# ScalarE instead of VectorE blanks the sums of two graph attentions, and the count stores are issued one group sooner

## The chip, the cores and the metric

The kernel runs on one core of one Trainium2 chip. The metric is the device time of one execution in microseconds (us). A core has TensorE (PE in the rows), VectorE (DVE), ScalarE (ACT), GpSimd (POOL) and SyncE (SP), each with its own instruction stream; they wait for each other on semaphores. Transfers run on 16 DMA engines, and here they are issued by SP (dense copies) and by POOL (gathers of single rows by an index).

## The reference, cut to what matters

Four graph networks run one after the other on the same 3125 nodes of 256 numbers, each followed by a residual sum and a layer norm. The first two are attentions over 53125 edges, sorted by their target node. For the first one, with `row` the source and `col` the target of an edge:

```python
scores = jnp.sum(Q[col] * (K[row] + rel), axis=-1) / np.sqrt(DK)
m = jax.ops.segment_max(scores, col, num_segments=N)
e = jnp.exp(scores - m[col])
denom = jax.ops.segment_sum(e, col, num_segments=N)
out = jax.ops.segment_sum((e / denom[col])[:, :, None] * V[row], col, num_segments=N)
x = _layernorm(x + out.reshape(N, 256) @ Wo.T + bo)
```

The second attention takes its scores from one number per node, head and side (`alpha_src[src] + alpha_dst[dst]`, then a leaky ReLU) instead of a product of rows, and has the same softmax and sums. The third and fourth network (five and three layers) sum over the same edges; this kernel does that as a product with a dense 3125 x 3125 matrix that counts the edges between each pair of nodes.

## The kernel before, in words

Both attentions are one function, `attend_edges`, called with `layer` 0 and 1. The edges stand in 416 chunks of 128, and eight chunks are a group, so there are `NG` = 52 groups. One turn of the loop over groups is called a tick here. For a group:

- POOL gathers the source rows of its 1024 edges, one indirect transfer per chunk, into one of four buffers (`from_src`, line 827). It may run ahead until all four buffers are in use.
- SP loads eight windows of target rows (`window`, line 807), two buffers. Ahead of each eight it reads eight start offsets into registers (line 800). From the third group on it also waits until PE has used the buffer.
- PE spreads the windows over the edges by a product with a one-hot matrix (`spread_windows`, line 987). VectorE turns the result into scores: in attention 0 it multiplies (`match`, line 850) and reduces (line 858), in attention 1 it reduces and adds the gathered part (`take_scores`, from line 864). Then it scans for the peaks (876, 879), builds the one-hot matrix of two groups later (840, 841), and subtracts (`shift_scores`, 889, 892).
- ScalarE takes the exponential (`weigh`, 1101, 1102). VectorE weights the rows by it (`weigh_rows`, 897, one tick later), and PE sums the 128 rows of each chunk (`sum_parts`, 1017, 1019) into one of three PSUM banks. ScalarE copies each bank into `sums` at the chunk's offset (`copy_sums`, line 1120) and the last two columns into `ends` (1122).

`sums` is 3 planes of 3712 columns, on 128 partitions. Chunks write 128 columns each at run-time offsets and may leave columns out, so `sums` has to be blank before the first copy. In attention 1 it lies in a part of `room`, and the rows show it by that name. Line 940 blanks it as one instruction on VectorE, after the first two one-hot matrices and some smaller memsets and ahead of the first scores.

Attention 1 also makes the count matrix (`adj`), in ticks 0 to 49. VectorE makes one-hot matrices of windows (`spot_windows`, 929, 931), PE multiplies them one tick later (1032), and ScalarE copies 160 results into `counts`, a buffer of two halves (1135). Sixteen halves are written in all. SP stores each to `adj` (line 795), and ScalarE waits before the first copy of a half until the store of the half two before it has landed. SP stands in the order of its loop: the windows of group g, then `store_halves(g)`, which issues the store of each half that falls to g:

```python
done = next(t for t in range(NG) if HG * (half + 1) <= NWG * (t + 1) // TICKS)
if g == min(NG - 1, done + 5):
```

`done` is the tick in whose turn VectorE makes the last one-hot matrices of the half. The halves come every three ticks, now and then four, and the last two are both issued at g = 51. An attention ends when every engine has passed a barrier; SP passes it when all stores have landed.

Of the kernel before, what the change touches and what calls it, by code (L numbers as in the profile page):

```python
# [11 lines left out]
ACT = mybir.ActivationFunctionType  # L12
AX_X = mybir.AxisListType.X

P = 128
# [3 lines left out]
KH = D // P  # L19
# [5 lines left out]
C = 416  # L25
G = 8
NG = C // G
# [3 lines left out]
PBUF = PARTS + P  # L31
# [50 lines left out]
def sems(nc, ctx, *names):  # L82

    made = [nc.alloc_semaphore(name=n) for n in names]
    ctx.used += made
    return made
# [619 lines left out]
def attend_edges(nc, keep, layer, by_src, by_part, ws, wd, scale, adj=None):  # L706
# [7 lines left out]
    with Phase(nc) as ctx:  # L714
# [57 lines left out]
        win_in = sems(nc, ctx, *(f"e{layer}_win_in{b}" for b in range(2)))  # L772
        spread = sems(nc, ctx, *(f"e{layer}_spread{s}" for s in range(2)))
        used = sems(nc, ctx, *(f"e{layer}_used{s}" for s in range(2)))
        whole_copied, blank = sems(nc, ctx, f"e{layer}_whole_copied", f"e{layer}_blank")
        spotted, counted, copied = sems(nc, ctx, *(f"e{layer}_{n}" for n in ("spotted", "counted", "copied")))
        half_out = sems(nc, ctx, *(f"e{layer}_half_out{i}" for i in range(2)))
        block = ctx.enter_context(nc.Block(f"edges{layer}"))
# [4 lines left out]
        def width_of(half):  # L783
            return AN - HALF if half % 2 else HALF

        @block.sync
        def _(sp):
            def store_halves(g):

                for half in range(NHALF):  # L790
                    done = next(t for t in range(NG) if HG * (half + 1) <= NWG * (t + 1) // TICKS)
                    if g == min(NG - 1, done + 5):
                        sp.wait_ge(copied, HG * (half + 1))
                        at = half % 2 * HALF
                        sp.dma_start(adj[half // 2][:, :, at:at + width_of(half)],
                                     counts[:, half % 2, :, 0:width_of(half)]).then_inc(half_out[half % 2], 16)

            def load_windows(it, b, again):
                g = RING * it + b
                starts = [sp.value_load(keep["offset"][0:1, bass.ds(g * G + j, 1)], min_val=0, max_val=PARTS) for j in range(G)]  # L800
                if again and layer == 0:

                    sp.wait_ge(spread[1], PAIRS // 2 * (g - 1))
                elif again:
                    sp.wait_ge(spread[b % 2], RING // 2 * it + b // 2)
                for j in range(G):
                    sp.dma_start(window[:, b % 2, j, :], by_part[bass.ds(starts[j], P), :]).then_inc(win_in[b % 2], 16)

            for b in range(RING):
                load_windows(0, b, b >= 2)  # L810
            for g in range(RING, NG):
                load_windows(g // RING, g % RING, True)
                if counting:
                    store_halves(g)
            if counting:
                for i in range(2):
                    sp.wait_ge(half_out[i], 16 * (NHALF // 2))
# [14 lines left out]
        def _(v):  # L832
# [104 lines left out]
            nc.vector.memset(small[:, :, :, COL_SIZE:SMALL], 1.0).then_inc(zeroed, 1)  # L937
            for s in range(BANKS):
                nc.vector.memset(part_ps[s][COL_SIZE:P, KH * ENDS:(KH + 1) * ENDS], 0.0).then_inc(blank, 1)
            nc.vector.memset(keep["sums"][:, :, :], 0.0).then_inc(zeroed, 1)  # L940
            v.wait_ge(zeroed, 3)
            if layer == 0:
                for pair in range(PAIRS):
                    match(0, pair)
# [143 lines left out]
        def _(act):  # L1088
            act.sem_inc(hot_copied, 1)

            def copy_turned(g):
                r = g % 2
                act.wait_ge(hot_turned, g + 1)
                nc.scalar.activation(onehot_t[:, r, :, :], hot_ps[:, :].rearrange("p (j e) -> p j e", j=G),
                                     ACT.Copy).then_inc(hot_copied, 1)

            def weigh(g):
                r = g % 2
                act.wait_ge(shift_done, g + 1)
                by_head = shifted[:, r, :].rearrange("p (j h) -> p j h", h=H)  # L1100
                nc.scalar.activation(share(r), by_head, ACT.Exp, scale=scale).then_inc(prob, 1)  # L1101
                nc.scalar.activation(small[:, r, :, 0:H], by_head, ACT.Exp, scale=scale).then_inc(prob_kept, 1)
# [42 lines left out]
            def tick_alpha(g):  # L1145
                copy_sums(g - 2, range(4, G))
                copy_counts(g - 1, 0, 1)
                copy_sums(g - 1, (0, 1))
                copy_counts(g - 1, 1, 2)
                if g + 2 < NG:  # L1150
                    copy_turned(g + 2)
                copy_sums(g - 1, (2,))
                copy_counts(g - 1, 2, 3)
                weigh(g)
                copy_sums(g - 1, (3,))
                copy_counts(g - 1, 3, 4)

            copy_turned(0)
            copy_turned(1)
            act.wait_ge(zeroed, 3)  # L1160
            for g in range(NG):
                if layer == 0:
                    tick_rows(g)
                else:
                    tick_alpha(g)
            copy_sums(NG - 2, range(4, G))
            copy_sums(NG - 1, range(G))

# [1957 lines left out]
```

## Time and profile before

| | |
|---|---|
| time, median of 3 runs | 2911.0 us (2905.76 to 2912.67) |
| profiled execution | 2911.57 us, span 2909.8 us |
| busy: PE, VectorE, ScalarE, POOL | 2641.3, 1567.8, 1086.8, 970.0 us |
| granted clock of TensorE, mean share | 0.956 |
| moved by DMA | 470.22 MB, 162 GB/s on the mean |

The profile is one execution; its span is what the trace covers, and 1.8 us of the time lie around it. Times in rows are us from the start of the span. A row of the timeline reads: start, duration, engine, line, operation, output<-inputs, shape, count, and in brackets how long the engine had been idle and what ended that. A duration can overlap the next instruction by some tens of ns.

### The profile page before, as it was taken

What the parts mean: (1) busy time and instruction counts of PE and PEld (TensorE: products, weight loads), DVE (VectorE), ACT (ScalarE), POOL (GpSimd) and SP (SyncE); (2) the same over time, 40 slices, a digit from 0 to 9 for tenths busy, and PEclk for the clock granted to TensorE, in tenths of its full rate; (3) what the DMA queues carried; (4) which work ended last, traced back from release to release, by engine and by line L of the source; (5) the groups of instructions that cost most, each with busy time, mean ns of one, the idle gap of its engine ahead of it and who ended that gap; (6) DMA issues with size and microseconds to landing.
All of it is one profiled execution on the core that took longest, in us unless ns stands there. A gap on an engine that the chain in (4) does not pass through costs nothing. (4 is left out here: it accounts for less than half of the span.)

```text
span 2909.8 us, 53292 instructions
## 1 busy us (share of the span) xinstructions
PE 2641.3 (91%) x17214; PEld 1918.8 (66%) x17214; DVE 1567.8 (54%) x2779; ACT 1086.8 (37%) x3021; POOL 970.0 (33%) x1020
## 2 busy tenths in 40 slices
PE   6789999998747888888799999999999989999998
PEld 4679999997636777777455555655556556565654
DVE  8689999995567888886721514215142151111123
ACT  1035555554426777776321304013040152021111
POOL 3577777772367777773400101001010000000000
PEclk8999999999769999999699999999999999999999
DMA  7799999992347988987554342543425143434342
GB/s 258 253 321 319 316 317 321 314 312 87 89 99 135 163 150 153 154 158 112 162 156 125 91 138 63 152 125 103 126 63 154 54 126 111 138 91 132 112 123 86
DMA packets 332505, 470.22 MB, mean 162 GB/s; under 512 B 155942, under 2 KB 243062, under 8 KB 331588
## 3 DMA queue, kind: packets, MB, share of 16 engines
q1 hardware_dynamic: 269364, 286.33, 38.1%
q0 software_dynamic: 59088, 176.67, 19.9%
q10 hardware_dynamic: 3776, 3.80, 0.4%
q8 instruction: 140, 2.29, 0.3%
q14 instruction: 137, 1.12, 0.1%
HBM read 412.95 MB, written 55.50 MB: 161 GB/s over the span
## 5 line engine op out<-in xcount | busy, mean ns | idle before, releaser
L2348 PE MATMUL sum_ps<-room,high 128*128 128x391 f16 x1900 | 470.3, 331 | 2.4 <-DVE z_t L2525 2.4
L2348 PE MATMUL sum_ps<-room,low 128*128 128x391 f16 x1824 | 454.1, 331 | 0.0
L827 POOL DMA_INDIRECT e_from_src<-vk,src x416 | 393.4, 946 | 141.0 <-issue 109.7
L827 POOL DMA_INDIRECT e_from_src<-val,src x416 | 393.5, 946 | 134.1 <-issue 107.3
L2746 PE MATMUL sum_ps<-room,high 128*128 128x391 f16 x1200 | 389.4, 329 | 0.5 <-DVE x L2890 0.5
L2746 PE MATMUL sum_ps<-room,low 128*128 128x391 f16 x1152 | 379.3, 329 | 0.0
L1017 PE MATMUL e_part_ps<-e_onehot,e_from_src 128*128 128x129 f32 x1664 | 288.7, 297 | 80.9 <-ACT ends L1122 71.6
L2525 DVE SCALAR_TENSOR_TENSOR z_t<-h_t,own,sum_ps 128x391 f32<-128x391 f32 x80 | 44.7, 618 | 483.9 <-PE sum_ps L2348 480.2
L1017 PEld LDWEIGHTS e_part_ps<-e_onehot,e_from_src 128*128 128x128 f32 x1664 | 225.7, 197 | 110.2 <-ACT ends L1122 97.7
L1120 ACT ACTIVATE sums<-e_part_ps 128x384 f32 x416 | 205.2, 493 | 231.1 <-PE e_part_ps L1019 203.4
L2416 POOL TENSOR_SCALAR h_t<-h_t 128x391 f32<-128x391 f32 x32 | 39.0, 1237 | 697.2 <-DVE h_t L2555 697.2
L1017 PE MATMUL e_part_ps<-x,e_from_src 128*128 128x129 f32 x1664 | 267.2, 283 | 1.7 <-DVE e_from_src L897 1.1
L2348 PEld LDWEIGHTS sum_ps<-room,high 128*128 128x128 f16 x1900 | 185.1, 98 | 126.3 <-issue 3.7
L2348 PEld LDWEIGHTS sum_ps<-room,low 128*128 128x128 f16 x1824 | 178.2, 98 | 127.7 <-issue 2.6
L2425 ACT ACTIVATE gin_y_t<-gin_proj_ps,gin_columns 128x391 f32<-128x391 f32 x80 | 47.0, 587 | 561.3 <-PE gin_proj_ps L2365 560.5
L1120 ACT ACTIVATE room<-e_part_ps 128x384 f32 x416 | 206.5, 496 | 124.4 <-PE e_part_ps L1019 59.1
L897 DVE TENSOR_TENSOR e_from_src<-e_from_src,e_fixed 128x2048 f32<-128x2048 f32 x104 | 237.3, 2282 | 15.4 <-ACT e_fixed L1101 15.4
L1017 PEld LDWEIGHTS e_part_ps<-x,e_from_src 128*128 128x128 f32 x1664 | 229.7, 191 | 20.1 <-DVE e_from_src L897 1.8
L987 PE MATMUL e_spread_ps<-e_window,x 128*128 128x256 f32 x832 | 214.4, 385 | 15.5 <-DMA e_window<-q_part 15.4
L2746 PEld LDWEIGHTS sum_ps<-room,high 128*128 128x128 f16 x1200 | 116.8, 97 | 80.3 <-issue 1.2
L987 PEld LDWEIGHTS e_spread_ps<-e_window,x 128*128 128x128 f32 x832 | 144.2, 193 | 34.2 <-DMA e_window<-q_part 12.8
L2746 PEld LDWEIGHTS sum_ps<-room,low 128*128 128x128 f16 x1152 | 112.3, 97 | 80.4 <-issue 2.1
(424 smaller groups left out, 4481.3 us busy)
## 6 DMA issues: line engine op xcount, KB each, us to landing
room<-adj SPq DMA_DIRECT2D x128, 977.5 KB, 4.8
e_window<-q_part SPq DMA_DIRECT2D x416, 128.0 KB
room<-adj SPq DMA_DIRECT2D x32, 488.8 KB
room<-adj SPq DMA_DIRECT2D x32, 391.0 KB
adj<-e_counts SPq DMA_DIRECT2D x8, 1250.0 KB
adj<-e_counts SPq DMA_DIRECT2D x8, 1193.8 KB
e_from_src<-vk,src POOLq DMA_INDIRECT x416
e_from_src<-val,src POOLq DMA_INDIRECT x416
```

What stands on the lines that cost most here:

```text
L827: nc.gpsimd.indirect_dma_start(from_src[:, b, j, :], None, by_src, bass.IndirectOffsetOnAxis(ap=keep["src"][:, g * G + j:g * G + j + 1], a ...
L897: nc.vector.tensor_tensor(from_src[:, b, :, 0:D].rearrange("p j (h d) -> p j h d", h=H), from_src[:, b, :, 0:D].rearrange("p j (h d) -> p ...
L987: mm = nc.tensor.matmul(to, onehot_t[:, r, j, :], window[:, r, j, :], start=True, stop=True)
L1017: nc.tensor.matmul(part_ps[s][:, k * ENDS:(k + 1) * ENDS], from_src[:, b, j, k * P:(k + 1) * P], onehot[:, b, j, :], start=True, stop=True)
L1120: nc.scalar.activation(keep["sums"][:, :, bass.ds(starts[j], P)], of[:, :, 0:P], ACT.Copy).then_inc(whole_copied, 1)
L2348: mm = nc.tensor.matmul(sum_ps[KH * n + m][:, 0:AN], part[:, t, m * P:(m + 1) * P], slab[s][:, n, k * AN:(k + 1) * AN], start=(t == 0 and ...
L2416: nc.gpsimd.tensor_scalar(h_t[:, 1, cols(b)], h_t[:, 1, cols(b)], 0.0, None, ALU.max).then_inc(floored, 1)
L2425: nc.scalar.activation((z_t if p else y_t)[:, m, cols(b)], proj_bank(p, v)[:, 0:AN], ACT.Identity, bias=columns[:, 3 * p, m:m + 1], scale= ...
L2525: nc.vector.scalar_tensor_tensor(out=z_t[:, m, cols(b)], in0=h_t[:, m, cols(b)], scalar=own[:, l:l + 1], in1=sum_ps[KH * n + m][:, 0:AN], ...
L2746: mm = nc.tensor.matmul(sum_ps[KH * n + m][:, 0:AN], part[:, t, m * P:(m + 1) * P], slab[s][:, n, k * AN:(k + 1) * AN], start=(t == 0 and ...
```

## The change

Blanking moves from VectorE to ScalarE, in three instructions of one plane each (`clear_sums`). They copy a zero, the last column of `once`, broadcast over 3712 columns. The first stands ahead of ScalarE's first one-hot copy, the second behind its second one, and the third at the end of tick 0, with a wait until all three are written. VectorE and ScalarE wait for two memsets instead of three. The stores of the counts are issued at `done + 4` instead of `done + 5`, so all but the last one stand one group sooner in SP's loop.

```diff
-        whole_copied, blank = sems(nc, ctx, f"e{layer}_whole_copied", f"e{layer}_blank")
+        whole_copied, blank, cleared = sems(nc, ctx, *(f"e{layer}_{n}" for n in ("whole_copied", "blank", "cleared")))
...
-                    if g == min(NG - 1, done + 5):
+                    if g == min(NG - 1, done + 4):
                         sp.wait_ge(copied, HG * (half + 1))
...
-            nc.vector.memset(keep["sums"][:, :, :], 0.0).then_inc(zeroed, 1)
-            v.wait_ge(zeroed, 3)
+            v.wait_ge(zeroed, 2)
...
+            def clear_sums(k):
+                nc.scalar.activation(keep["sums"][:, k, :], keep["once"][:, C:C + 1].to_broadcast([P, PBUF]),
+                                     ACT.Copy).then_inc(cleared, 1)
+
+            clear_sums(0)
             copy_turned(0)
             copy_turned(1)
-            act.wait_ge(zeroed, 3)
+            clear_sums(1)
+            act.wait_ge(zeroed, 2)
             for g in range(NG):
                 if layer == 0:
                     tick_rows(g)
                 else:
                     tick_alpha(g)
+                if g == 0:
+                    clear_sums(KH)
+                    act.wait_ge(cleared, KH + 1)
```

The start of attention 1 on ScalarE before the change: the one-hot copies of three groups stand together, and the first copy of counts follows the two exponentials of tick 0.

```order
L1087 UNCONDITIONAL_BRANCH
L1094 ACTIVATE e_onehot_t<-e_hot_ps 128x1024 x3
L1101 ACT_TABLE_LOAD
L1101 ACTIVATE e_fixed<-e_shifted 128x64
L1102 ACTIVATE e_small<-e_shifted 128x8x8
L1135 ACTIVATE e_counts<-e_count_ps,whole 128x25x20
```

The same place after the change (line numbers of the changed file are one less here).

```order
L1086 UNCONDITIONAL_BRANCH
L1158 ACTIVATE room<-once 128x3712
L1093 ACTIVATE e_onehot_t<-e_hot_ps 128x1024 x2
L1158 ACTIVATE room<-once 128x3712
L1093 ACTIVATE e_onehot_t<-e_hot_ps 128x1024
L1100 ACT_TABLE_LOAD
L1100 ACTIVATE e_fixed<-e_shifted 128x64
L1101 ACTIVATE e_small<-e_shifted 128x8x8
L1158 ACTIVATE room<-once 128x3712
L1134 ACTIVATE e_counts<-e_count_ps,whole 128x25x20
```

The three blanking copies now stand on ScalarE, one of them between tick 0's exponentials and its first copies out of PSUM; attention 0 has the same order without counts.

The end of attention 1 on SP before the change, behind the offsets of group 51: the last windows, then the stores of the last two halves, one behind the other.

```order
L807 ISA
L807 DMA e_window<-alpha_part 128x24
L807 ISA
L807 DMA e_window<-alpha_part 128x24
L795 DMA adj<-e_counts 3200x1x200
L795 DMA adj<-e_counts 3200x1x191
L714 UNCONDITIONAL_BRANCH
```

The place after the change to which the first of these two stores has gone: behind the windows of group 50, ahead of the offsets of group 51.

```order
L807 ISA
L807 DMA e_window<-alpha_part 128x24
L807 ISA
L807 DMA e_window<-alpha_part 128x24
L795 DMA adj<-e_counts 3200x1x200
L800 TENSOR_LOAD offset
L800 ISA x2
L800 TENSOR_LOAD offset
L800 ISA x2
```

The store of half 14 stands ahead of group 51's sixteen register reads and eight windows now; only half 15 is left at the end.

## Rows read from the trace of the kernel before

**Rows 1.** Instructions of the gathers (L827): durations ns, first and last start us.

```profile
L827 POOL DMA_INDIRECT e_from_src<-vk,src x416: 940/946/962, 133.4 to 652.3; - x139
L827 POOL DMA_INDIRECT e_from_src<-val,src x416: 941/946/992, 824.9 to 1344.1; - x139
```

**Rows 2.** Instructions of line 940, the same columns, and the idle time before them.

```profile
L940 DVE MEMSET sums<- x1: 9338/9338/9338, 139.6 to 139.6; 128x11136 f32 x1
L940 DVE MEMSET room<- x1: 9338/9338/9338, 831.1 to 831.1; 128x11136 f32 x1
...
  issue: 4.6, 2
```

**Rows 3.** Timeline of VectorE, start of attention 0 and two ticks near its end.

```profile
148.98 0.69 DVE L850 TENSOR_TENSOR e_from_src<-e_from_src,e_spread_ps 128x512 f32<-128x512 f32 x1
...
643.56 0.69 DVE L850 TENSOR_TENSOR e_from_src<-e_from_src,e_spread_ps 128x512 f32<-128x512 f32 x1 [0.65 <-PE e_spread_ps L987]
...
653.50 0.69 DVE L850 TENSOR_TENSOR e_from_src<-e_from_src,e_spread_ps 128x512 f32<-128x512 f32 x1 [0.65 <-PE e_spread_ps L987]
```

**Rows 4.** Timeline of PE, start of attention 0.

```profile
146.25 5.76 PE L987 MATMUL e_spread_ps<-e_window,x 128*128 128x256 f32 x16 [8.54 <-DMA e_window<-q_part]
...
164.18 2.07 PE L987 MATMUL e_spread_ps<-e_window,x 128*128 128x256 f32 x4 [3.85 <-DMA e_window<-q_part]
```

**Rows 5.** Timeline of SP's issues, start of attention 0: windows of group 2.

```profile
155.11 3.95 SPq L807 DMA_DIRECT2D e_window<-q_part  x8
```

**Rows 6.** Timeline of VectorE, start of attention 1.

```profile
840.51 0.36 DVE L864 TENSOR_REDUCE e_spread_score<-e_turn_ps 128x64 f32<-128x192 f32 x1
...
856.43 0.36 DVE L864 TENSOR_REDUCE e_spread_score<-e_turn_ps 128x64 f32<-128x192 f32 x1 [0.35 <-DMA e_from_src<-val,src]
```

**Rows 7.** Timeline of POOL: last gather of group 2, attention 1.

```profile
853.69 0.95 POOL L827 DMA_INDIRECT e_from_src<-val,src  x1 [0.30 <-issue]
```

**Rows 8.** Groups by line of ScalarE: count | busy us, mean ns.

```profile
L569 ACT ACTIVATE pr_part_room<-first 128x3328 bf16<-128x3328 f32 x1 | 3.0, 2977 | 2.4 <-DVE first L347 2.4
```

**Rows 9.** Timeline of ScalarE: ticks 0 and 1 of attention 0, tick 0 of attention 1.

```profile
161.50 0.25 ACT L1102 ACTIVATE e_small<-e_shifted 128x64 f32<-128x64 f32 x1
170.36 0.49 ACT L1120 ACTIVATE sums<-e_part_ps 128x384 f32 x1 [8.61 <-PE e_part_ps L1019]
...
848.12 0.24 ACT L1102 ACTIVATE e_small<-e_shifted 128x64 f32<-128x64 f32 x1
...
852.40 0.49 ACT L1120 ACTIVATE room<-e_part_ps 128x384 f32 x1 [2.36 <-PE e_part_ps L1019]
```

**Rows 10.** Timeline of SP's issues, end of attention 1.

```profile
1310.32 0.56 SPq L795 DMA_DIRECT2D adj<-e_counts  x1
...
1327.30 3.94 SPq L807 DMA_DIRECT2D e_window<-alpha_part  x8
...
1339.83 0.56 SPq L795 DMA_DIRECT2D adj<-e_counts  x1
```

**Rows 11.** Timeline of VectorE, ticks 48 to 51 of attention 1.

```profile
1325.98 0.36 DVE L864 TENSOR_REDUCE e_spread_score<-e_turn_ps 128x64 f32<-128x192 f32 x1 [0.72 <-DMA e_from_src<-val,src]
...
1344.83 0.34 DVE L864 TENSOR_REDUCE e_spread_score<-e_turn_ps 128x64 f32<-128x192 f32 x1
...
1349.92 0.42 DVE L876 TENSOR_TENSOR_SCAN e_fixed<-link,e_turn_ps 64x128 f32<-64x128 bf16 x1 [2.04 <-PE e_turn_ps L995]
...
1356.20 0.36 DVE L864 TENSOR_REDUCE e_spread_score<-e_turn_ps 128x64 f32<-128x192 f32 x1 [3.50 <-DMA e_from_src<-val,src]
```

**Rows 12.** Timeline of ScalarE, end of attention 1.

```profile
1361.15 0.49 ACT L1120 ACTIVATE room<-e_part_ps 128x384 f32 x1 [1.95 <-PE e_part_ps L1019]
...
1374.04 0.17 ACT L1122 ACTIVATE ends<-e_part_ps 128x6 f32<-128x6 f32 x1
```

**Rows 13.** Waits of SP in 820:1380: us in total, times, longest.

```profile
SPq L817 <- DMA adj<-e_counts: 12.7, 1, 12.7
```

**Rows 14.** Waits of ScalarE in 820:1376, the same columns.

```profile
ACT e_counts L1135 <- DMA adj<-e_counts: 14.4, 5, 8.7
```

## Prediction

> **What bounds the kernel now.** The change touches the two attentions alone, so I read each attention by asking which engine sets its pace, then what its first ticks wait for, then what its last ticks wait for.
>
> The instructions of the gathers come first [rows 1]. In attention 1 POOL starts its first gather at 824.9 us and its 416th at 1344.1: 519.2 us over 415 steps, 1.251 us each. In attention 0 it is (652.3 - 133.4) / 415 = 1.250. One gather is 0.946 us, and the rest of the step is POOL's own issue gap. So POOL is never held up for long by a full buffer, and a group of eight costs it 10.0 us. Attention 1 follows this: whenever the other engines are quicker than 10.0 us per tick they run into a gather that has not landed. Its end is the landing of the last gathers plus a tail. Attention 0 has a pace of its own: VectorE's `match` of successive ticks, still waiting for PE both times, stands 653.50 - 643.56 = 9.94 us apart [rows 3]. PE is the limit there, by a hair, and whatever delays PE's start delays the end.
>
> **The blanking on VectorE, attention 0.** The memset takes 9.338 us [rows 2], and the first `match` starts right behind it at 148.98 with no idle time before it [rows 3]. It looks as if 9.3 us could be had. But the first `match` needs PE's spread of the first windows, and PE could not start that before 146.25, when the windows landed [rows 4]. So the first `match` can come forward by at most 148.98 - 146.25 = 2.7 us. And this does not carry on: PE waits again, 3.85 us, for the windows of group 2, which land at 164.18 [rows 4]. Are these windows late because their buffer was freed late? SP issues them from 155.11 on [rows 5]; the buffer was free when PE had spread group 0, at the latest at 146.25 + 5.76 = 152.0 [rows 4]. SP was still reading its eight offsets then, so it was SP's own loop that set 155.11. From 164.18 on the ticks run at PE's pace. The memset ends 15 us before that. Gain: bounds 0 and 2.7 us, and I take 0, because two waits with no VectorE in them lie behind it.
>
> **The same, attention 1.** The memset is 9.338 us again [rows 2], and the first scores start at 840.51 right behind [rows 6]. But group 2's scores at 856.43 wait for a gather [rows 6]: POOL's last gather of that group starts at 853.69 and ends at 854.64 [rows 7], 1.8 us before. No VectorE is in this chain, and two ticks have taken up all of the memset. With both idle stretches ahead of the memsets (4.6 us for the two [rows 2]) the most that could be had in this attention is 9.3 + 2.3 = 11.6 us; I take 0.
>
> **The blanking on ScalarE.** The trace before has no copy of 3712 columns on ScalarE. The nearest row is one of 3328 columns at 2977 ns [rows 8], 0.895 ns a column, so 3.3 us each and 10 us per attention. Below it cannot be nothing; above, I allow double, should the broadcast source or the f32 output cost more. The first two copies stand in the time in which ScalarE waits for the one-hot matrices and PE for the windows of 146.25 [rows 4]. The third stands behind tick 0's exponentials. In attention 0 these end at 161.75, and the first copy of sums starts at 170.36 after 8.61 us of idle time [rows 9]; 3.3 us fit, and so do 6.6. Queued behind the clearing wait are the reads of the offsets and the first copies of sums, and PE waits for these only from its fourth chunk on, since it has three banks. In attention 1 the exponentials end at 848.36 and only 2.36 us of idle time stand right ahead of the first copy of sums [rows 9], so that copy may be some 1 us late, or 4 us with the doubled price, and the gather wait of the next ticks takes that up. Cost: 0.
>
> **The stores.** A store is issued behind the eight windows of its group. That of half 13 is issued at 1310.32 and that of half 14 at 1339.83 [rows 10]. Each makes the gathers behind it late: group 48's scores start only at 1325.98 and group 51's only at 1356.20, both released by a gather [rows 11], 15.7 and 16.4 us behind the store. Group 51's last gather was started at 1344.1 [rows 1], so it needed 11 us to land instead of the 1.8 us of a quiet stretch. The last tick of all thus waits 3.50 us for a store that stands in its way [rows 11].
>
> The Trainium skill (DMA: Bandwidth & Descriptors, Queues, rings and completion order) says that each DMA engine takes turns between the queues that have work, packet by packet. By that rule a gather would pass between the pieces of a store and land almost in time, and where the store stands would be worth nothing. The rows just named speak against it.
>
> With `done + 4` the store of half 14 goes out behind the windows of group 50, at 1327.30 + 3.94 = 1331.2 [rows 10], 8.6 us sooner. Now it meets the last gathers of group 50 (the last one starts 10 us before 1344.1, so at 1334.1, some 3 us behind the store). By the two distances above, tick 50 starts at 1331.2 + 15.7 to 16.4 = 1346.9 to 1347.6 instead of 1344.83 [rows 11]. Group 51's last gather starts 13 us behind the store and should land in time. Tick 50 lasts until its last subtraction; before, tick 51 could have started 3.50 us before 1356.20, at 1352.70, so tick 50 took 7.9 us, and 2.04 of these were a wait for PE [rows 11]. If that wait absorbs the later start, tick 51 starts at 1352.7 as VectorE was free before; if it absorbs nothing, at 1347.6 + 7.9 = 1355.5. Either way it gains: 0.7 to 3.5 us.
>
> The tail passes this on only in part. Behind tick 51 ScalarE starts again at 1361.15, after 1.95 us of idle time, and copies to 1374.2 [rows 12]. Work that comes sooner can pull this forward by the 1.95 us, and no more, because ScalarE is busy before that. So the gain at the end is 0.7 to 2 us, and I take 1.5. The last store stays where it was: SP waits 12.7 us for it [rows 13], issued about 1357, so it lands at about 1370 and has 4 us left to ScalarE's end. The 14.4 us in which ScalarE waited for stores, 8.7 of them at once [rows 14], should vanish, but they lie inside an attention that POOL paces.
>
> **The sum.** Attention 0: 0 - 0. Attention 1: 0 for the blanking, -1.5 for the stores. The profiled execution took 2911.57 us, so 2910.1; it stands 0.6 above the median of 2911.0, so the median to expect is **2909.5 us**.
>
> **Rivals.**
>
> - *The blanking is on the path after all.* Then both attentions start up to 11.6 us sooner, 23.3 in all: 2887.7 us. For it speaks that VectorE has no idle time behind either memset; against it the two waits for windows and gathers, which contain no VectorE. Chance 0.05.
> - *The lost stall is kept as a gain.* If the 8.7 us that ScalarE no longer waits early in attention 1 carried through, 2902.3 us. Against it: POOL did not slow down there, 1.251 us a gather throughout. Chance 0.05.
> - *Slower, by the place of the store.* Tick 50 is made late, and tick 51 keeps its whole distance from it, 1356.20 - 1344.83 = 11.4 us, because the same backlog of transfers now also holds group 51 or its windows, which stand behind the store in SP's order. Then tick 51 starts at 1347.6 + 11.4 = 1359.0, 2.8 us late: 2913.8 us. It decides from the point at which tick 50 lasts longer than 1356.20 - 1347.6 = 8.6 us. Chance 0.12.
> - *Slower, by ScalarE.* If one blanking copy took more than the 8.6 us of idle time, attention 0's PE would pay for the rest one to one; to lose 9 us a copy would have to take some 17 us, five times the nearest row. About 2920 us. Chance 0.03.
> - *The stores move and nothing follows*, by the rule of taking turns, or because the tail hangs on ScalarE alone: 2911.0 us. Chance 0.1.
>
> **How the numbers follow.** My forecast, a gain of 0.7 to 3.5 us at the end of attention 1, has 0.65. About 0.3%, 8.7 us, is what a measurement of this kernel can tell from no change; the three runs before lie 6.9 us apart. The forecast, no effect and the late store all lie within it, which is 0.87. Faster by more takes the first rival and half of the second, 0.08; slower by more takes the ScalarE rival and a little for what I overlook, 0.05. For the range I take the forecast's and the two middle rivals' bounds, 2907.5 to 2913.8, and widen them by what single runs scatter below and above the median, 5.2 and 1.7 us: 2902 to 2915.5.
>
> **What would show it.** Right: VectorE is idle where line 940 stood, and the steady ticks of attention 0 still begin behind PE's wait for windows at about 164; the blanking copies take about 3.3 us each; POOL's first and 416th gather stand where they stood within 1 us, in both attentions; ScalarE's waits for stores fall from 14.4 us to near nothing; tick 50 of attention 1 waits for a gather and tick 51 does not. Wrong: an end of attention 0 that moves by more than 3 us, a blanking copy above 7 us, or a last tick that waits for gathers again.

## The result and the profile after

| | before | after |
|---|---|---|
| time, median of 11 runs each | 2907.56 us (2902.67 to 2912.67) | 2921.85 us (2915.06 to 2927.07) |
| profiled execution, span | 2911.57, 2909.8 us | 2924.08, 2922.3 us |
| busy: PE, VectorE, ScalarE, POOL | 2641.3, 1567.8, 1086.8, 970.0 us | 2649.9, 1548.3, 1107.6, 971.3 us |

The ratio is 1.0045, 95% interval 1.0032 to 1.0058: the change made the kernel some 13 us slower. The forecast was 2909.5.

First the instructions of the gathers, of the blanking and of the copies of sums after the change (durations in ns, first and last start in us):

```profile
L827 POOL DMA_INDIRECT e_from_src<-vk,src x416: 942/949/963, 135.3 to 655.5; - x139
L827 POOL DMA_INDIRECT e_from_src<-val,src x416: 942/949/997, 826.9 to 1355.4; - x139
L1158 ACT ACTIVATE sums<-once x3: 3283/3287/3296, 134.8 to 163.6; 128x3712 f32<-128x3712 bf16 x3
L1158 ACT ACTIVATE room<-once x3: 3278/3287/3296, 826.3 to 849.0; 128x3712 f32<-128x3712 bf16 x3
L1119 ACT ACTIVATE room<-e_part_ps x416: 484/493/552, 853.5 to 1386.9; 128x384 f32 x139
```

and the same copies of sums before:

```profile
L1120 ACT ACTIVATE room<-e_part_ps x416: 479/492/570, 852.4 to 1373.7; 128x384 f32 x139
```

Compare stretches, not places. The 416 gathers of attention 0 take 520.2 us (518.9 before, [rows 1]), and from its first gather to that of attention 1 it is 691.6 us, 691.5 before. In attention 1 the gathers take 528.5 us instead of 519.2, and from the first gather to the last copy of sums it is 1386.9 - 826.9 = 560.0 us instead of 1373.7 - 824.9 = 548.8. So 11.2 us of the span's 12.5 were lost inside attention 1, and 9.3 of them before the last gather.

The blanking did what was forecast. VectorE's first `match` now waits for PE, PE still waits for the windows of group 2 (to 166.18, with a first gather 1.9 us later than before; [rows 4] have 164.18), and ScalarE keeps 5.47 us of its idle time. The timeline of VectorE after, at the first `match`:

```profile
150.39 0.69 DVE L850 TENSOR_TENSOR e_from_src<-e_from_src,e_spread_ps 128x512 f32<-128x512 f32 x1 [11.18 <-PE e_spread_ps L986]
```

that of PE, at group 2's windows:

```profile
166.18 2.08 PE L986 MATMUL e_spread_ps<-e_window,x 128*128 128x256 f32 x4 [3.88 <-DMA e_window<-q_part]
```

and that of ScalarE, from the third blanking copy to the first copy of sums:

```profile
163.62 3.28 ACT L1158 ACTIVATE sums<-once 128x3712 f32<-128x3712 bf16 x1
172.37 0.49 ACT L1119 ACTIVATE sums<-e_part_ps 128x384 f32 x1 [5.47 <-PE e_part_ps L1018]
```

Where the stores act, the waits of attention 1 show it (us in total, times, longest). After:

```profile
POOL e_from_src L827 <- PE e_part_ps L1018: 28.4, 65, 2.9
PE e_turn_ps L986 <- DMA e_window<-alpha_part: 21.5, 10, 5.8
```

and before:

```profile
POOL e_from_src L827 <- PE e_part_ps L1019: 19.3, 63, 0.4
PE e_turn_ps L987 <- DMA e_window<-alpha_part: 14.3, 11, 6.2
```

PE waits 7.2 us more for windows, and POOL now waits up to 2.9 us for a buffer that PE has not finished with; before, its longest such wait was 0.4 us. Windows are SP's work. The instructions of its issues before:

```profile
L807 SPq DMA_DIRECT2D e_window<-alpha_part x416: 327/333/1417, 828.8 to 1339.5; - x139
```

and after:

```profile
L807 SPq DMA_DIRECT2D e_window<-alpha_part x416: 328/333/2672, 830.7 to 1355.8; - x139
```

One issue takes 0.33 us, but the longest took 2.67 us. The store issues mark SP's turns. Before, the store of half 0 is issued at 906.23 (SP's timeline, below) and that of half 14 at 1339.83 [rows 10], 43 groups later: 10.08 us a group, no quicker than POOL's 10.0.

```profile
906.23 0.61 SPq L795 DMA_DIRECT2D adj<-e_counts  x1
...
1028.09 0.56 SPq L795 DMA_DIRECT2D adj<-e_counts  x1
1035.90 22.49 SPq L807 DMA_DIRECT2D e_window<-alpha_part  x24
```

After, in the same timeline, it is (1343.99 - 898.00) / 43 = 10.37 us a group, and SP falls behind POOL:

```profile
898.00 0.62 SPq L795 DMA_DIRECT2D adj<-e_counts  x1
...
989.39 0.56 SPq L795 DMA_DIRECT2D adj<-e_counts  x1
996.99 22.56 SPq L807 DMA_DIRECT2D e_window<-alpha_part  x24
1019.60 0.56 SPq L795 DMA_DIRECT2D adj<-e_counts  x1
1027.37 25.73 SPq L807 DMA_DIRECT2D e_window<-alpha_part  x24
...
1083.77 0.75 SPq L795 DMA_DIRECT2D adj<-e_counts  x1
1091.75 27.63 SPq L807 DMA_DIRECT2D e_window<-alpha_part  x24
...
1250.77 0.56 SPq L795 DMA_DIRECT2D adj<-e_counts  x1
1258.55 25.90 SPq L807 DMA_DIRECT2D e_window<-alpha_part  x24
...
1343.99 0.56 SPq L795 DMA_DIRECT2D adj<-e_counts  x1
```

Read the rows of 24 windows: behind the store of 989.39 three groups of windows took 22.56 us, behind those of 1019.60, 1083.77 and 1250.77 they took 25.73, 27.63 and 25.90. All other such rows after the change lie between 21.92 and 23.13 us, and all of those before between 21.89 and 23.49. So three of the fourteen stores hold SP by 3 to 5 us more than the others, and they carry nearly the whole loss.

### The profile page after: what moved, and what is told of

It reads as the page before. It is cut to its first block and busy times, and to the rows that moved or that the text cites. A ratio compares the mean times of both kernels' runs of the same rounds, so it can differ in the third digit from the quotient of the medians.

```text
span 2922.3 us, 53297 instructions
## 1 busy us (share of the span) xinstructions
PE 2649.9 (91%) x17214; PEld 1929.6 (66%) x17214; DVE 1548.3 (53%) x2777; ACT 1107.6 (38%) x3027; POOL 971.3 (33%) x1020
## 5 line engine op out<-in xcount | busy, mean ns | idle before, releaser
L827 POOL DMA_INDIRECT e_from_src<-val,src x416 | 394.4, 948 | 142.3 <-issue 106.7
L827 POOL DMA_INDIRECT e_from_src<-vk,src x416 | 394.5, 948 | 141.8 <-issue 110.5
L1016 PE MATMUL e_part_ps<-e_onehot,e_from_src 128*128 128x129 f32 x1664 | 294.8, 302 | 75.0 <-ACT ends L1121 65.9
L2356 PEld LDWEIGHTS sum_ps<-room,low 128*128 128x128 f16 x1824 | 178.3, 98 | 127.7 <-issue 2.6
L1018 PE MATMUL e_part_ps<-e_onehot,e_small 128*65 128x129 f32 x832 | 166.9, 284 | 0.0
L986 PEld LDWEIGHTS e_spread_ps<-e_window,x 128*128 128x128 f32 x832 | 144.7, 194 | 33.4 <-DMA e_window<-q_part 12.4
```

The source lines that it names most:

```text
L827: nc.gpsimd.indirect_dma_start(from_src[:, b, j, :], None, by_src, bass.IndirectOffsetOnAxis(ap=keep["src"][:, g * G + j:g * G + j + 1], a ...
L986: mm = nc.tensor.matmul(to, onehot_t[:, r, j, :], window[:, r, j, :], start=True, stop=True)
L1016: nc.tensor.matmul(part_ps[s][:, k * ENDS:(k + 1) * ENDS], from_src[:, b, j, k * P:(k + 1) * P], onehot[:, b, j, :], start=True, stop=True)
L1018: nc.tensor.matmul(part_ps[s][0:SMALL, KH * ENDS:(KH + 1) * ENDS], small[:, r, j, :], onehot[:, b, j, :], start=True, stop=True).then_inc( ...
L2356: mm = nc.tensor.matmul(sum_ps[KH * n + m][:, 0:AN], part[:, t, m * P:(m + 1) * P], slab[s][:, n, k * AN:(k + 1) * AN], start=(t == 0 and ...
```

## The experiments

All in one table. "Stretch" is from the first gather to the last copy of sums in attention 1, "SP" the time per group between the stores of halves 0 and 14 (43 groups apart, 44 in e3 and e13, 42 in e4 and e14), "packets" what the last experiment is about, and L807 the longest window issue. All but the ratio is read from the one profiled execution of a run, whose time can lie off the median (e4's is 10 us above it, e15's 9 us below). e5 and e6 ran once and write most of the counts behind the attention, so that only their stretch is read.

| run | ratio to before, interval | stretch us | SP us a group | packets | L807 us |
|---|---|---|---|---|---|
| before | | 548.8 | 10.08 | 0 | 1.42 |
| after | 1.0045 (1.0032, 1.0058) | 560.0 | 10.37 | 9 | 2.67 |
| e1 | 0.9993 (0.9981, 1.0005) | 547.0 | 10.05 | 0 | 1.59 |
| e2 | 1.0043 (1.0027, 1.0059) | 559.0 | 10.35 | 7 | 2.76 |
| e3 | 0.9987 (0.9975, 0.9999) | 548.0 | 10.03 | 2 | 1.46 |
| e4 | 1.0040 (1.0024, 1.0056) | 566.2 | 10.54 | 8 | 4.43 |
| e5 | (not compared) | 540.9 | | | 1.80 |
| e6 | (not compared) | 543.6 | | | 1.70 |
| e7 = after | 1.0037 (1.0021, 1.0052) | 557.4 | 10.35 | 7 | 2.92 |
| e8 | 0.9999 (0.9984, 1.0013) | 551.3 | | | 1.76 |
| e9 | 1.0028 (1.0014, 1.0043) | 555.4 | | | 1.50 |
| e10 | 1.0001 (0.9990, 1.0013) | 552.1 | 10.17 | 1 | 1.53 |
| e11 | 1.0207 (1.0190, 1.0223) | 610.0 | 11.34 | | 2.05 |
| e12 | 1.0171 (1.0148, 1.0193) | 602.5 | 11.23 | | 6.68 |
| e13 | 1.0012 (0.9996, 1.0027) | 557.6 | 10.28 | 4 | 5.43 |
| e14 | 1.0021 (1.0008, 1.0035) | 557.2 | 10.32 | 3 | 2.84 |
| e15 | 1.0010 (0.9998, 1.0021) | 550.9 | | | 2.07 |
| e16 | 1.0030 (1.0017, 1.0043) | 558.0 | | | 1.49 |
| e17 | 1.0032 (1.0019, 1.0046) | 554.4 | 10.09 | 1 | 1.67 |
| e18 | 1.0022 (1.0006, 1.0039) | 557.5 | 10.31 | 5 | 2.59 |

**Which part: e1, e2.** The change with its stores put back, and the kernel before with the stores alone moved:

```diff
-                    if g == min(NG - 1, done + 4):
+                    if g == min(NG - 1, done + 5):
```


> The blanking part alone: ScalarE blanks in three parts, the stores stay at done + 5. Three theories for the 14 us that the change lost, all of them in attention 1, where POOL's 416 gathers took 528.5 us instead of 519.2. Theory A (all stores): a store one group sooner meets SP's loop badly, SP issues the windows later, and the engines behind fall back until POOL waits for a free buffer. Theory B (blanking): ScalarE's copies upset the first ticks. Theory C (the first store alone): the early stall of 9 us that the change took away kept the later ticks in a better order. A and C expect no change here, 0 to 3 us from the kernel before, 416 gathers of attention 1 in about 519 us. B expects some 14 us more.

> The stores alone: all at done + 4, VectorE blanks with one memset as before. A and C expect the loss here, about 14 us more than before (2921 to 2922 us), with POOL's gathers of attention 1 in about 528 us and SP's 51 steps between the windows of group 0 and group 51 near 521 us instead of 507. B expects a time within 3 us of the kernel before.

The blanking is worth nothing either way; the stores are the whole loss.

**Which stores: e3, e4, e13, e14.** Only the first store at `done + 4`; all but the first; halves 0 to 7; halves 8 to 15:

```diff
-                    if g == min(NG - 1, done + 4):
+                    if g == min(NG - 1, done + (4 if half < 8 else 5)):
```


> Only the store of half 0 at done + 4, the other fifteen at done + 5, VectorE blanks. C expects most of the loss here, 8 to 14 us more than before, since the early stall is gone. A expects little, within 3 us, perhaps a gain of 1 us, as fifteen stores stand where they stood. B expects no change.

> The store of half 0 at done + 5 as before, all others at done + 4, VectorE blanks. A expects most of the loss, 10 to 14 us more than before. C expects no loss, within 3 us, since the early stall is back (ScalarE waits some 9 us for the first store once). B expects no change.

> The changed kernel, but only the first eight count stores stand behind the fourth group, the other eight behind the fifth as before. Theory R (SyncE's loop takes 507 us where GpSimd's gathers take 519, so that some 12 us of stalls are free, and only what the sixteen stores add beyond that shows): half the stores add 7 us to the loop, within the room; attention 1 in 548 to 552 us, kernel 2906 to 2913 us. Theory L (each early store costs its share, 11.4 us over 15): attention 1 in 553 to 556 us, kernel 2914 to 2917 us. Theory T (only the last stores hurt, by meeting the last gathers): as before, 2905 to 2910 us.

> The changed kernel, but only the last eight count stores stand behind the fourth group, the first eight behind the fifth as before. Theory R: as with the first eight, attention 1 in 548 to 552 us, kernel 2906 to 2913 us. Theory L: half the loss, kernel 2914 to 2917 us. Theory T (the last stores meet the last gathers): the whole loss, attention 1 in 557 to 562 us, kernel 2918 to 2925 us.

The first store is innocent. In e13's profile, which leaves the last stores in place, SP is slow all the same; but its time cannot be told from the kernel before, so that the last stores are cleared by the profile alone. Between a threshold and a share per store the two runs do not decide: e13's median, 2911.86, lies in the threshold's range, e14's, 2917.07, just above the share's.

**The bytes: e5, e6.** One row block of 25, or eight columns of 200, per store:

```diff
-                        sp.dma_start(adj[half // 2][:, :, at:at + width_of(half)],
+                        sp.dma_start(adj[half // 2][:, 0:1, at:at + width_of(half)],
...
```


> The changed kernel, but each of the 16 count stores takes only the first of the 25 row blocks at its place (128 pieces of 400 B in place of 3200); the rest of the table is written after attention 1, from whatever the count buffer then holds, so the values of the other 24 blocks are not the reference's and the whole time is some 200 us longer. Only attention 1 is read: from its first gather to its last copy of sums (548.7 us before, 560.1 after). Theory A (while a store drains, SyncE's own window issues are held, and the windows come late): no issue of L807 over 0.6 us, the 416 gathers in 519 us, the stretch in 545 to 549 us. Rival P (the place in the order costs by itself, through SyncE's wait for the counts or the extra store ahead of the last windows, whatever its size): 557 to 562 us, as after.

> The changed kernel, but each count store takes only the first 8 columns of all 25 row blocks at its place: still 3200 pieces, of 16 B in place of 400; the other columns are written after attention 1 from whatever the count buffer then holds, so their values are not the reference's and the whole time is longer. Only attention 1 is read. Theory A with the number of pieces as what holds SyncE: longest issue of L807 2 us or more, stretch 555 to 562 us. Theory A with the bytes as what holds it: issues below 0.6 us, stretch 545 to 549 us. Rival P (the place alone): 557 to 562 us, and then the run with few pieces is as long too.

Without their bytes the stores at the new place cost nothing: the gathers take 519 us, and the attention is even 5 to 8 us shorter than before, all of it behind the start of the last gather (22.0 and 24.6 us to the last copy of sums, 29.6 before). The pieces' number is not what hurts. The expected bound of 0.6 us for an issue was wrong: single issues of 1.7 us occur even so.

**SP's loop: e10, e11, e12, e15.** e10 lets the old place wait for one more tick's counts; e11 adds two dropped reads to each of SP's loops; e12 puts the store between the fourth and fifth window; e15 takes four of eight reads away from the changed kernel.

```diff
-                        sp.wait_ge(copied, HG * (half + 1))
+                        sp.wait_ge(copied, min(HG * NHALF, NWG * (done + 2) // TICKS))
```
```diff
+                if counting:
+                    for j in range(2):
+                        sp.value_load(keep["offset"][0:1, bass.ds(g * G + j, 1)], min_val=0, max_val=PARTS)
```
```diff
                 for j in range(G):
+                    if counting and again and j == G // 2 and g >= RING:
+                        store_halves(g)
...
```


> The kernel before, with its stores behind the fifth group, but each store also waits until ScalarE has copied the counts of the tick after the half's last one (the data stored are the same). So the store stands in the old place of SyncE's order, and is as close behind ScalarE's copies as the changed kernel's. Theory W (SyncE's small waits for the copies tie its loop to ScalarE, and it loses the lead that it needs): attention 1 in 555 to 562 us, kernel 2916 to 2926 us. Theory D (the order decides: four groups or five between counts and store, and which windows stand behind it): attention 1 in 547 to 550 us, kernel 2904 to 2912 us.

> The kernel before, but SyncE reads two more offsets in each group of attention 1 and drops them, some 0.9 us more in each of its 52 loops (8 reads and 8 window issues take 8.5 us now). If SyncE's loop has no more room than its 10 us a group against GpSimd's 9.98 (A's premise): SyncE then needs some 10.8 us a group, attention 1 lasts 30 to 40 us longer, kernel 2937 to 2950 us. If SyncE has room (its windows wait in any case, and A's stalls do harm by something else, such as held gathers): attention 1 within 5 us, kernel 2904 to 2915 us.

> The kernel before, but each count store stands between the fourth and the fifth of the eight windows of its fifth group: half a group sooner than before, half a group later than in the change. Theory W (the waits for the copies): SyncE comes there with its counts copied, so no wait, and the time is as before: attention 1 in 547 to 551 us, kernel 2904 to 2912 us. Theory D with a cost that grows with the place: half the loss, attention 1 in 553 to 556 us, kernel 2913 to 2916 us.

> The changed kernel, all stores behind the fourth group, but in attention 1 SyncE reads only every other offset and uses each for two windows, so half of the windows hold the rows of a neighbouring chunk: their bytes and number are the same, the values of attention 1 are not the reference's. SyncE's loop becomes some 2 us a group shorter (e11 showed about 1.2 us for two reads less overlap). Theory R: with that room the same stores cost nothing: attention 1 in 541 to 550 us, kernel 2899 to 2909 us. If the early stores do harm by holding the gathers themselves, whatever SyncE's pace: attention 1 in 555 to 562 us, kernel 2916 to 2924 us.

e10 cost nothing (its stretch of 552.1 us lies between the two expectations), but its new waits were short, so it says little on long ones. The change has no long ones either. SP's own waits for counts, before:

```profile
SPq L795 <- ACT e_counts L1135: 16.2, 1, 16.2
```

and after:

```profile
SPq L795 <- ACT e_counts L1134: 15.4, 5, 13.6
```

The longest is each time that for the last half, and the four others that the change brought are 15.4 - 13.6 = 1.8 us in all, of the 12.4 that SP lost. e11 is the plain one: two reads made each loop 11.34 - 10.08 = 1.26 us longer (0.9 expected), and the attention grew by 61 us (30 to 40 expected). SP has no room. The kernel before shows the same in another way: among SP's waits in attention 1 there is none for a window buffer. e12 missed both expectations by some 45 us: half-way between two places that differ by 13 us it cost 50. A window issued right behind a store is held up to 6.68 us; in the old order eight reads stand in between, and the longest issue is 1.42. With half the reads (e15, 2911.65 us, 2899 to 2909 expected) SP has room and waits 105.0 us for PE, and the kernel loses 6 us at most instead of 9 to 17. But SP's turns came at other times too, and only 1 of e15's 15 stores meets a packet (see below), so e15 does not tell the room from the packets. The wait in SP's own view:

```profile
SPq L808 <- PE e_turn_ps L987: 105.0, 39, 9.1
```

**Other ways to store: e8, e9, e16.** Each store in two parts, 12 blocks at `done + 4` and 13 at `done + 5`; the stores issued by ScalarE; both together.

```diff
-                    if g == min(NG - 1, done + 4):
+                    for part, later in ((slice(0, NT // 2), 4), (slice(NT // 2, NT), 5)):
+                        if g == min(NG - 1, done + later):
...
```


> The changed kernel, but each store is cut in two by row blocks: 12 of the 25 behind the fourth group, 13 behind the fifth. Theory A with the length of a store as what hurts (SyncE is held only once a long store is still draining when the next windows are issued): issues of L807 below 1 us, attention 1 in 545 to 552 us, kernel 2903 to 2912 us, though SyncE issues twice as many stores (15 x 0.6 us more). If each store costs SyncE a fixed stall of some 3 us, whatever its size, twice the stores cost 40 us more in SyncE's loop: attention 1 590 to 605 us, kernel 2950 to 2965 us.

> The changed kernel, but ScalarE issues each count store itself, at the end of its tick in which the half's last counts are copied, so that no window stands behind a store in SyncE's order; the stores are the same, and come at about the same time. (The run e7_scalar_queue was meant to be this; by a mistake it held the changed kernel unaltered, and so is a second measurement of that.) Theory A with SyncE's order as the place (what hurts is that windows stand behind the store): issues of L807 all below 0.6 us, attention 1 from first gather to last copy of sums in 541 to 549 us, kernel 2900 to 2908 us. Theory A with the DMA engines as the place (whoever issues the store, its pieces fill the engines that windows and gathers need): attention 1 in 555 to 562 us, kernel 2917 to 2926 us.

> A version that might beat both: ScalarE blanks the sums as in the change and issues the count stores as in e9, each cut in two by row blocks (12 behind the tick that completes its counts, 13 behind the next; for the half before the last, one tick later, clear of the last gathers). SyncE's loop holds no store at all. Theory A with R: no window late, gathers in 519 us, and a tail as short as before or shorter: attention 1 in 541 to 549 us, kernel 2899 to 2909 us. If ScalarE's 32 issues delay its copies, or stores meet the last gathers as in e9: attention 1 over 553 us, kernel 2913 us or more.

Cutting the stores takes the loss away and gives nothing beyond it, though issues of up to 1.76 us remain (below 1 expected). (The run e7 was the changed kernel itself.) With ScalarE as the issuer SP has room and no issue above 1.5 us (0.6 expected), and the gathers of e9 take 520.5 us; yet the last copy comes 35 us behind the last gather instead of 29.6, and the kernel still loses 8 us. So windows and gathers behave as the theory of SP's order has it, but e9's stretch lies in the range of the other theory. e16 stores half 14 a tick later, clear of the last gathers, and its tail is 37.1 us. What that tail consists of is open. No version is clearly faster than the kernel before; e3 comes nearest, with an interval of 0.9975 to 0.9999.

**What makes some stores hold SP: e17, e18.** In the DMA view q1 carries SP's copies, q0 POOL's gathers, and q8 and q14 are called instruction queues. The view from 0.5 us ahead of a store to 11.5 us behind it, for the slow store of 1019.60 after the change:

```profile
q1 hardware_dynamic: 3504, 1.24, 94.3%
q0 software_dynamic: 147, 0.42, 17.0%
q8 instruction: 1, 0.02, 0.7%
q14 instruction: 1, 0.01, 0.5%
```

and for the store of 1028.09 before, with no row of q8 or q14:

```profile
q1 hardware_dynamic: 3436, 1.22, 105.4%
q0 software_dynamic: 101, 0.29, 11.0%
```

The table's "packets" counts the stores, of the first 15, that have a q8 packet (16 KB) in these 12 us. e17 and e18 lengthen PE's program, which moves the packets and not one store in SP's order:

```diff
+            if counting:
+                for i in range(167):
+                    pe.sem_inc(pe_passed, 1)
             pe.wait_ge(ident_set, 1)
```


> The changed kernel, and TensorE passes 167 empty instructions (increments of a semaphore that nobody waits for) at the start of attention 1, where it idles 20 us; the stores stay behind the fourth group. In the traces, the five stores of the changed kernel that drain longest (16.7 to 18.6 us) are the five in which a 16-KB packet of the instruction queue lands 0.9 to 1.3 us behind the store; before, none lands in a store's first 12 us. These packets come about every 15.3 us, 256 instructions of 64 B, which is TensorE's pace (some 165 a tick). 167 instructions move them by about one tick against the stores, to where they stood before. Theory F (the instruction packet at the head of a store makes the long store, which holds SyncE's windows): no such packet in the first 3 us of the stores, L807's longest below 2 us, attention 1 in 547 to 553 us, kernel 2904 to 2913 us. If the packets only accompany it: attention 1 in 556 to 562 us, kernel 2916 to 2924 us.

> The kernel before, its stores behind the fifth group, and TensorE passes 89 empty instructions at the start of attention 1, which moves its instruction packets by about one tick the other way against the stores (256 less 167), to where they stand in the changed kernel. Theory F: packets of the instruction queue land in the first 3 us of several stores, L807's longest is over 2 us, attention 1 in 556 to 562 us, kernel 2916 to 2926 us, with not one store moved. If the packets only accompany it: attention 1 in 547 to 551 us, kernel 2904 to 2912 us.

The packets moved with PE's program, and SP's loop answered as theory F has it. With the changed stores and the packets moved off (e17), 1 of 15 is left and SP is back at (1335.98 - 902.16) / 43 = 10.09 us a group, by its timeline:

```profile
902.16 0.62 SPq L795 DMA_DIRECT2D adj<-e_counts  x1
...
1335.98 0.56 SPq L795 DMA_DIRECT2D adj<-e_counts  x1
```

With the old stores and the packets moved on (e18, 89 increments in place of 167), 5 of 15 meet one, SP needs (1347.85 - 904.60) / 43 = 10.31, the longest issue is 2.59 us, and the kernel loses 2 to 11 us; SP's timeline:

```profile
904.60 0.61 SPq L795 DMA_DIRECT2D adj<-e_counts  x1
...
1282.76 0.56 SPq L795 DMA_DIRECT2D adj<-e_counts  x1
1290.66 27.47 SPq L807 DMA_DIRECT2D e_window<-alpha_part  x24
...
1347.85 0.56 SPq L795 DMA_DIRECT2D adj<-e_counts  x1
```

The time of e17 did not follow: 2904 to 2913 was expected and 2917.2 came, a ratio that cannot be told from the changed kernel's. The empty instructions were slow, so that PE's first product came 851.12 - 827.97 = 23 us later than after the change, and SP waited once at the start, as its own waits show:

```profile
SPq L807 <- PE e_turn_ps L989: 8.5, 1, 8.5
```

A loop without room carries such a delay to the end. The store of half 0 stands 902.16 - 824.8 = 77.4 us behind the first gather, after the change 898.00 - 826.9 = 71.1: 6.3 us, and the stretch is 5.6 us over that of before. That fits, but that this wait is the whole rest was not tested. In e18 PE began 838.95 - 826.06 = 12.9 us later than before, and SP has no such wait.

Of the narrower form of F, a packet in a store's first 3 us, several were expected in e18, and only one store has it. But this is the store of 1282.76, with the one long row of windows (27.47 us), and it carries 35.42 - 3 x 10.08 = 5.2 of the 9.7 us that SP lost there. The traces of the twelve runs that have the count allow the same store by store, over the three or four groups from one store to the next. With a q8 packet from 0.5 us ahead of a store to 3 us behind it, 11 of 20 stores took over 11 us a group (mean 11.04); with one later, up to 11.5 us behind it, 2 of 23 (10.35); with none 1 of 123 (10.11). A q14 packet in the first 3 us, and none of q8 in the 12, leaves the mean at 10.12 (25 stores). So a q8 packet at the head of a store makes a long hold likely and not certain, and one long hold (e13, behind 1225.89) came without a packet.

## Why the prediction was wrong

**The blanking** (both attentions, VectorE's gain 0, ScalarE's cost 0): right in each step. The copies take 3.287 us (3.3 forecast), PE's wait for group 2's windows is still there, and e1 measured no difference.

**The stores**: this is the step that failed. It said that a store one group sooner matters where it meets the last gathers, and priced half 14 alone, at -1.5 us. The other fourteen stores moved as well and were given no price, because "Attention 1 follows" POOL. But that a wait-free POOL takes 10.0 us a group does not say that others have room: SP needed 10.08, with its eight reads, eight issues and a third of a store per group. The prediction had itself found SP's loop to set a start in attention 0 (155.11), and did not ask the same of attention 1. The moved stores made it 10.37: over 43 groups 445.99 - 433.60 = 12.4 us, the size of the loss. At the end things went as told only in part. The tail, in which the 1.5 us were to be had, grew: from the start of the last gather to the last copy of sums it is 1386.9 - 1355.4 = 31.5 us instead of 29.6. ScalarE's waits for stores did vanish, and the last tick no longer waits for gathers (last starts of scores, VectorE, after; those of before are in [rows 11]):

```profile
1347.13 0.34 DVE L864 TENSOR_REDUCE e_spread_score<-e_turn_ps 128x64 f32<-128x192 f32 x1
1359.13 0.34 DVE L864 TENSOR_REDUCE e_spread_score<-e_turn_ps 128x64 f32<-128x192 f32 x1
1365.86 0.35 DVE L864 TENSOR_REDUCE e_spread_score<-e_turn_ps 128x64 f32<-128x192 f32 x1
```

None of the three waits for a gather, not even tick 50, whose late gathers the step counted on: by then the ticks were behind the gathers. What the step read from the rows, that a store holds gathers issued behind it, stands: in the DMA view before, from 1342 to 1349, POOL issues three gathers while the store of 1339.83 drains, and there is a row of q1 and none of q0.

```profile
q1 hardware_dynamic: 2276, 0.91, 133.8%
...
e_from_src<-val,src POOLq DMA_INDIRECT x3
```

The test named in advance, POOL's 416th gather within 1 us of its place, failed: in attention 1 it starts 11.3 us later, 9.3 of them within the attention, and that pointed to the right stretch. In attention 0 it is 3.2 us later, of which 1.9 came ahead of the first gather; e10, whose start is that of the kernel before, has its first gather at 135.3 too.

**The rivals.** "Slower, by the place of the store" had the right order of things (windows that stand behind the store in SP's order), but only for the last two ticks, 2.8 us. The loss was in the whole attention, so its price was some five times too small. The kept stall, the blanking on the path, ScalarE as the cause and "nothing follows" all fell.

**What is shown and what is open.** Shown: the stores' place alone (e1, e2), through their bytes (e5, e6), by way of SP's loop, which has no room (e11). That instruction packets at the stores slow SP's loop is shown for the loop, in one profile each way: with PE's program lengthened it went from 10.37 to 10.09 (e17) and from 10.08 to 10.31 (e18). Over the twelve runs that have the count it sorts them: 10.03 to 10.17 us a group with at most two, 10.28 to 10.54 with three or more. In kernel time only e18 bears it out; e17's delayed start may hide what it gave back. So four or five groups is no rule in these runs; the new place happened to stand where PE's packets fall. Open: how one packet of 16 KB makes a store hold the windows and why not each does, why e9 still loses at its end, and whether the loss grows with each store.

## What to carry to other kernels

Before a transfer is moved in a queue, work out the period of that queue's own loop, reads and issues included, and set it against the engine that paces: a loop within 1% of the pacing engine is on the path, even if it never shows as busy. When many transfers move, price them all and not the one at the end. A place that was found by trial may hold only by its phase against something that nobody placed, here the loading of another engine's instructions. Fewer reads (e15) and cut stores (e8) took the loss away at the new place; that they hold at any phase was not tested.

## What was not expected of the hardware

A window issued right behind a store of 1250 KB occupied SP for up to 6.68 us instead of 0.33 (e12). Gathers issued behind such a store moved nothing for 7 us (the view of 1342 to 1349 above). An empty increment on PE was not free: 78 of them (167 less 89) delayed PE's first product by 851.12 - 838.95 = 12.2 us, by estimate 0.16 us each. PE's timeline in e17:

```profile
851.12 1.01 PE L968 MATMUL e_hot_ps<-e_ident,e_onehot 128*128 128x128 bf16 x8 [45.57 <-issue]
```

and in e18:

```profile
838.95 1.01 PE L969 MATMUL e_hot_ps<-e_ident,e_onehot 128*128 128x128 bf16 x8 [33.69 <-issue]
```
